# v's projection in pairs with its weight halves side by side, h's weights formed with fewer copies, identity products in the tail

## The reference

```python
v = relu(x @ Wv + bv); q = relu(x @ Wq + bq); k = relu(x @ Wk + bk)
att = softmax(q @ k.T * mask - NEG * (1 - mask))
x1 = layernorm(x + relu((att @ v) @ Wo + bo))

h = x1 @ W_w.T + W_b
e, f = h @ a1, h @ a2
u = adj * exp(e[:, None] + f[None, :] + a_b)
out = layernorm(x1 + (u / u.sum(-1)) @ h)
```

## Time and profile before

| | us |
|---|---|
| median of three runs | 425.09 |
| lowest, highest | 424.24, 425.4 |
| the profiled execution | 424.09 |
| its span on the core | 422.4 |
| TensorE / VectorE / ScalarE / GpSimd busy | 396.3 / 348.4 / 336.8 / 266.7 |

### The profile page before, as it was taken

The page is one execution under the profiler, slowest core; times in us unless marked ns, Lnnn a source line. Parts: engine busy times, 40 slices in busy tenths (PEclk is TensorE's granted clock), DMA queues, the critical chain, the costliest instruction groups (busy, mean ns, idle before and its releaser), DMA issues.

```text
span 422.4 us, 8762 instructions
## 1 busy us (share of the span) xinstructions
PE 396.3 (94%) x2812; PEld 367.5 (87%) x2812; DVE 348.4 (82%) x1002; ACT 336.8 (80%) x642; POOL 266.7 (63%) x230
## 2 busy tenths in 40 slices
PE   8789999999999999999999999999999999998580
PEld 7668998899999999999999999999999989988480
DVE  4595789879869896989869996989969999898755
ACT  5375767998789896998789987998789788985753
POOL 2453446456709698497929697496929893751862
PEclk9889999999999999999999999999999999999666
DMA  8940472626781657726792657726592768226661
GB/s 290 372 151 2 139 238 71 229 60 215 276 298 52 222 190 252 285 67 215 270 326 73 225 204 257 264 81 219 199 330 71 248 184 267 100 83 184 209 174 50
DMA packets 37868, 80.71 MB, mean 191 GB/s; under 512 B 2752, under 2 KB 19264, under 8 KB 37824
## 3 DMA queue, kind: packets, MB, share of 16 engines
q1 hardware_dynamic: 37680, 80.03, 55.1%
q10 hardware_dynamic: 144, 0.14, 0.2%
HBM read 75.96 MB, written 4.19 MB: 190 GB/s over the span
## 4 chain that ended last, share of the span: by engine, by line
PE 76%; DVE 11%; ACT 3%; issue 3%; DMA 2%; POOL 1%; ACTq 0%; DVEq 0%; POOLq 0%
PE pt_ps L1415 11%; PE m_ps L1463 10%; PE av_ps L1427 7%; PE av_ps L1428 7%; PE av_ps L1429 7%; PE s_ps L1356 6%; PE s_ps L1358 6%; PE s_ps L1357 6%; PE m_ps L1363 4%; PE m_ps L1356 3%; PE m_ps L1358 3%; PE m_ps L1357 3%; DVE prob L920 3%; DMA adjt_in<-in_adj_t_dram 2%; PE m_ps L1364 2%
## 5 line engine op out<-in xcount | busy, mean ns | idle before, releaser
L622 ACT ACTIVATE prob_th<-pt_ps 128x512 fp32r<-128x512 f32 x128 | 74.5, 593 | 30.8 <-PE pt_ps L1415 30.4
L928 DVE TENSOR_TENSOR prob_tl<-pt_ps,prob_th 128x512 fp32r<-128x512 f32 x128 | 85.7, 682 | 16.2 <-ACT prob_th L622 15.8
L920 DVE CUSTOM_DVE_ANT_0 prob<-s_ps,penalty 128x1024 f32<-128x1024 f32 x64 | 78.1, 1220 | 16.4 <-issue 6.5
L614 ACT ACTIVATE prob<-prob,neg_max 128x1024 f32<-128x1024 f32 x64 | 73.5, 1149 | 14.9 <-DVE neg_max L920 14.9
L379 POOL TENSOR_SCALAR penalty<-adj_in 128x1024 bf16<-128x1024 f32 x64 | 66.6, 1053 | 15.7 <-DVE neg_max L920 9.1
L1415 PE MATMUL pt_ps<-ident,prob 128*128 128x128 f32 x512 | 74.7, 275 | 0.0
L1427 PE MATMUL av_ps<-prob_th,vh 128*128 128x256 f32 x256 | 74.4, 291 | 0.0
L1429 PE MATMUL av_ps<-prob_th,vl 128*128 128x256 f32 x256 | 72.4, 283 | 0.0
L1428 PE MATMUL av_ps<-prob_tl,vh 128*128 128x256 f32 x256 | 72.4, 283 | 0.0
L572 ACT ACTIVATE adj_t<-adjt_in 128x1024 fp32r<-128x1024 f32 x58 | 61.1, 1054 | 9.2 <-DMA adjt_in<-in_adj_t_dram 7.5
L1415 PEld LDWEIGHTS pt_ps<-ident,prob 128*128 128x128 f32 x512 | 60.1, 142 | 7.1 <-issue 0.4
(11 more groups left out here) (132 smaller groups left out, 928.4 us busy)
## 6 DMA issues: line engine op xcount, KB each, us to landing
adj_in<-in_adj_dram SPq DMA_DIRECT2D x64, 512.0 KB, 5.1
adjt_in<-in_adj_t_dram SPq DMA_DIRECT2D x64, 512.0 KB, 4.3
xt_in<-in_x_t_dram SPq DMA_DIRECT2D x16, 256.0 KB, 4.2
x_in<-in_x_dram SPq DMA_DIRECT2D x8, 512.0 KB, 4.7
out_dram<-out_sb SPq DMA_DIRECT2D x14, 256.0 KB, 5.4
out_dram<-out_sb SPq DMA_DIRECT2D x4, 128.0 KB, 1.8
wb<-in_pack_b_dram SPq DMA_DIRECT2D x1, 320.0 KB, 4.1
wa<-in_pack_a_dram ACTq DMA_DIRECT2D x1, 132.0 KB, 3.7
```

Source lines behind the costliest of these rows:

```text
L614: sc.activation(prob[i % 2][:, :], prob[i % 2][:, :], ACT.Exp, bias=neg_max[:, i:i + 1], scale=-1.0, accum_out=row_sum[b % 2][:, i:i + 1]) ...
L622: sc.activation(prob_th[n % 2][:, tiles(k), (i % 2) * P:(i % 2 + 1) * P], pt_ps[k][:, :].rearrange("p (c n) -> p c n", n=P), ACT.Copy).the ...
L920: v.tensor_tensor_reduce(out=prob[i % 2][:, :], in0=s_ps[:, :, :].rearrange("p a n -> p (a n)"), in1=penalty[:, n % RING, :], scale=-1.0, ...
L928: v.tensor_tensor(prob_tl[n % 2][at], pt_ps[k][:, :].rearrange("p (c n) -> p c n", n=P), prob_th[n % 2][at].bitcast(F32), ALU.subtract).th ...
```

## The change

- v's projection works with `product_side_by_side` on four banks of two blocks each, instead of two banks of four blocks with three matmuls per block. VectorE's `v_out` adds bias to the low half (into `v_low`) and then the sum of both into the bank, and a new `v_relu` on ScalarE writes `vf` from the bank. v is now the reference's, so `bo_full` is bo itself, and the third product of `form_w1`, `minus_bv` and `bv_wide` are gone.
- The identity is built inside `rhs1`; `w1h` and `w1l` are formed straight from the bank.
- `hold_clock` issues six products of the identity with itself, at two places of TensorE's tail.
- The orders of all five queues and of the three banks are written anew for head, pass and tail. x is loaded for batch p in pass p rather than a pass ahead.

```diff
-            def project_v(b, k):
-                pe.wait_ge(*lower(xtl_done, b, k))
-                vv = shared("v", b, k)
-                for c in range(TH):
-                    t = k * TH + c
-                    last = product(blk(vv, c), (blk(xth, t), blk(xtl, t)), (wvh, wvl))
+            def project_v(b, j):
+                pe.wait_ge(*lower(xtl_done, b, j // 2))
+                vv = shared("v", b, j)
+                for c in range(2):
+                    t = 2 * j + c
+                    last = product_side_by_side(vv[:, c * PAIR:(c + 1) * PAIR], (blk(xth, t), blk(xtl, t)), flat(w_hl[:, 2, :, :]), D)
                 last.then_inc(v_full, 1)
...
-                v.tensor_tensor(half(vf, k)..., bank["v", b, k]..., rows(minus_bv[:, :], TH), ALU.max).then_inc(v_evac, 1)
+                v.tensor_tensor(v_low[:, :, :], vv[:, :, 1, :], rows(bv_row, 2), ALU.add).then_inc(v_biased, 1)
+                dve.wait_ge(v_biased, TH * b + j + 1)
+                v.tensor_tensor(vv[:, :, 0, :], vv[:, :, 0, :], v_low[:, :, :], ALU.add).then_inc(v_summed, 1)
...
+            def v_relu(b, j):
+                wait(act, vl_done, 2 * (b - 1) + j // 2 + 1)
+                act.wait_ge(v_summed, TH * b + j + 1)
+                sc.activation(vf[:, j * PAIR:(j + 1) * PAIR]..., vv[:, :, 0, :], ACT.Relu).then_inc(v_evac, 1)
...
             def place_rhs1():
-                dve.wait_ge(ident_ok, 2)
-                v.tensor_copy(rhs1[:, 0:D], ident[:, :]).then_inc(rhs_ok, 1)
+                dve.wait_ge(wa_arrived, 16)
                 v.tensor_copy(rhs1[:, D:E1], wa[:, A1:A2 + 1]).then_inc(rhs_ok, 1)
                 v.tensor_copy(wb_wide[:, :], wa[:, WB:WB + 1].broadcast_to([P, P])).then_inc(rhs_ok, 1)
-                v.tensor_copy(bv_wide[:, :], wa[:, BV:BV + 1].broadcast_to([P, P])).then_inc(rhs_ok, 1)
...
             def split_w1():
-                v.tensor_copy(w1f[:, :], av_ps[:, 0:E1]).then_inc(w1_ok, 1)
+                v.tensor_copy(w1h, av_ps[:, 0:E1]).then_inc(w1_ok, 1)
                 v.tensor_copy(wb_row[:, :], av_ps[:, E1:E1 + D]).then_inc(w1_ok, 1)
                 v.tensor_copy(beta2[:, :], av_ps[:, E1 + D:2 * E1]).then_inc(w1_ok, 1)
-                v.tensor_tensor(bo_full[:, :], av_ps[:, 2 * E1:2 * E1 + D], bo_row, ALU.add).then_inc(w1_ok, 1)
-                v.tensor_copy(w1h, w1f[:, :]).then_inc(w1_ok, 1)
+                v.tensor_tensor(w1l, av_ps[:, 0:E1], w1h.bitcast(F32), ALU.subtract).then_inc(w1_ok, 1)
...
+            def hold_clock():
+                pe.wait_ge(ptl_done, 2 * T * B - 1)
+                for _ in range(HOLD):
+                    pe.matmul(pt_ps[0][:, 0:P], ident, ident, start=True, stop=True)
...
             def head():        # TensorE
                 project_q(0, 0)
                 project_k(0, 0)
                 project_k(0, 1)
-                project_q(0, 1)
+                form_w1()
                 project_v(0, 0)
                 project_v(0, 1)
-                form_w1()
+                project_q(0, 1)
                 scores(0, 0)
-                project_v(1, 0)
+                project_v(0, 2)
+                project_k(1, 0)
                 scores(0, 1)
...
             def head():        # VectorE
                 split_qk()
                 first_x_lo(0)
                 first_x_lo(1)
+                place_rhs1()
                 split_vo()
...
-                split_w1()
                 mask_max(0, 2)
...
                 mask_max(0, 3)
+                split_w1()
+                v_out(1, 1)
...
             def tail():        # TensorE
+                transpose_x1(LAST, 0)
+                attend(LAST, 3)
                 project_h(LAST, 0)
                 project_h(LAST, 1)
+                aggregate(LAST - 1, 6)
+                aggregate(LAST - 1, 7)
                 project_h(LAST, 2)
+                hold_clock()
+                project_out(LAST, 3)
                 project_h(LAST, 3)
                 transpose_x1(LAST, 1)
...
                 aggregate_early(0)
                 aggregate_early(1)
+                hold_clock()
                 aggregate_early(2)
```

More of the change, by code:

```diff
@@ L754, in batch_pass @@
-                prob_hi(p, 2, 0)
-                probs(p, 3)
+                k_out(p + 1, 0)
                 if there(p - 2):
                     round_adj(p - 2, 5)
+                q_hi(p + 1, 0)
+                prob_hi(p, 2, 0)
+                if there(p - 2):
+                    round_adj(p - 2, 6)
+                probs(p, 3)
+                k_out(p + 1, 1)
                 prob_hi(p, 2, 1)
                 if there(p - 2):
-                    round_adj(p - 2, 6)
+                    round_adj(p - 2, 7)
@@ L789, in batch_pass @@
+                prob_hi(p, 6, 1)
                 probs(p, 7)
-                if there(p + 2):
-                    x_hi(p + 2, 1)
-                prob_hi(p, 6, 1)
-                g_hi(p - 1, 0)
+                g_hi_den(p - 1)
+                v_relu(p + 1, 2)
             def tail():
-                exp_ef(LAST - 2, 1)
+                av_hi(LAST - 1, 2)
+                g_hi(LAST - 2, 1)
+                prob_hi(LAST - 1, 7, 0)
+                q_out(LAST, 1)
+                v_relu(LAST, 3)
@@ L893, in _, with v_out @@
             v = nc.vector
-            def v_out(b, k):
-                wait(dve, vl_done, 2 * (b - 1) + k + 1)
-                dve.wait_ge(v_full, 2 * b + k + 1)
-                v.tensor_tensor(half(vf, k).rearrange("p (t d) -> p t d", d=D),
-                                bank["v", b, k][:, :].rearrange("p (t d) -> p t d", d=D),
-                                rows(minus_bv[:, :], TH), ALU.max).then_inc(v_evac, 1)
+            def v_out(b, j):
+                if b == 0 and j == 0:
+                    dve.wait_ge(wb_arrived, 16)
+                wait(dve, v_summed, TH * b + j)
+                dve.wait_ge(v_full, TH * b + j + 1)
+                vv = bank["v", b, j][:, :].rearrange("p (t a d) -> p t a d", a=2, d=D)
+                v.tensor_tensor(v_low[:, :, :], vv[:, :, 1, :], rows(bv_row, 2), ALU.add).then_inc(v_biased, 1)
+                dve.wait_ge(v_biased, TH * b + j + 1)
+                v.tensor_tensor(vv[:, :, 0, :], vv[:, :, 0, :], v_low[:, :, :], ALU.add).then_inc(v_summed, 1)
             def first_x_lo(k):
@@ L1129, in batch_pass @@
             def batch_pass(p):
+                if there(p - 2):
+                    g_lo_den(p - 2)
                 if there(p - 3):
@@ L1284, in tail @@
                 agg_out(LAST - 1, 1)
+                shift_mean0(LAST, 0)
+                agg_out(LAST - 1, 2)
+                prob_lo(LAST, 6, 1)
+                agg_out(LAST - 1, 3)
+                prob_lo(LAST, 7, 0)
+                av_lo(LAST, 2)
+                agg_out(LAST - 1, 4)
+                prob_lo(LAST, 7, 1)
                 o_out(LAST, 2)
                 residual0(LAST, 2)
+                agg_out(LAST - 1, 5)
+                x1_lo(LAST, 0)
+                h_out(LAST, 0)
@@ L1560, in batch_pass @@
                 transpose_p(p, 0, 1)
+                if there(p - 2):
+                    aggregate(p - 2, 0)
                 attend(p - 1, 3)
-                project_k(p + 1, 0)
                 scores(p, 2)
@@ L1576, in batch_pass @@
                 transpose_p(p, 2, 0)
-                scores(p, 4)
                 transpose_p(p, 2, 1)
-                attend(p, 0)
-                if there(p - 2):
-                    aggregate(p - 2, 3)
+                project_k(p + 1, 1)
                 if there(p - 2):
                     aggregate(p - 2, 4)
+                scores(p, 4)
+                if there(p - 2):
+                    aggregate(p - 2, 5)
                 transpose_p(p, 3, 0)
                 if there(p - 2):
-                    aggregate(p - 2, 5)
+                    aggregate(p - 2, 6)
@@ L1587, in batch_pass @@
                 if there(p - 2):
-                    aggregate(p - 2, 6)
+                    aggregate(p - 2, 7)
+                project_v(p + 1, 0)
+                project_v(p + 1, 1)
+                scores(p, 5)
                 transpose_p(p, 3, 1)
                 transpose_x1(p - 1, 0)
-                scores(p, 5)
+                attend(p, 0)
                 transpose_p(p, 4, 0)
-                if there(p - 2):
-                    aggregate(p - 2, 7)
-                transpose_p(p, 4, 1)
@@ L1605, in batch_pass @@
                 transpose_p(p, 5, 1)
[L1606 removed]
+                project_h(p - 1, 7)
                 scores(p, 7)
[L1608 removed]
+                project_out(p, 0)
+                project_v(p + 1, 2)
                 transpose_p(p, 6, 0)
+                transpose_p(p, 6, 1)
+                project_v(p + 1, 3)
+                attend(p, 2)
                 project_q(p + 1, 1)
[L1611 to L1612 removed]
```

663 lines of the change are left out of this document (321 added, 342 removed), and 9 rows, old and new, of tables (HEAD_SLOTS, PASS_SLOTS).

## The result

The changed kernel takes 419.85 us (median of four runs, 418.63 to 420.71) against 424.95 of the kernel before on the same chip: ratio 0.9879, 95% interval 0.9847 to 0.9912. Forecast were 412.5 and a range up to 419.5. It is faster, by 5.1 us instead of 12.6 (424.95 and 425.09 as the start), and 0.35 us outside the range. The profiled execution is the slowest of the four (420.71, span 419.0); a second one of the same kernel, in the experiments, has a span of 417.7.

A forecast was written before the change was run, and what follows sets the result against it. TensorE's instruction count times spacing was taken to bound the middle passes, with idling and half speed in the head. 424.1 - 7.5 (head) - 5.0 (passes) - 0 (tail) = 411.6, plus 1.0 for the median, said as 412.5; range 407 to 419.5.

The forecast's parts named there:

- The head, both steps: Start to pass 1: first scores 3.6 us earlier, then 3.9 us less from there to pass 1; 7.5 in all.
- the second wait: Head, TensorE's 2.1 us wait for a mask-and-maximum result; what is left of 3.4 us lost to half speed comes behind it.
- v's products: Passes 1 to 6 on TensorE: 0.46 us per bank, 0.84 less per batch, 5.0 us in all, range 3.7 to 5.9.
- So I cost them at nothing: Passes: VectorE's and ScalarE's 1.5 us more each priced at 0 while TensorE bounds, up to 1.0 us per pass for the range.
- rival A: Passes: denser VectorE and ScalarE hold TensorE up by 1 us in each, 418.5 us; chance 0.17.
- The sum of VectorE: VectorE's busy time per pass: 1.5 us more for v's operations, to 42.5 us.
- Pass 1: First of the six passes that form v of later batches: 40.3 us forecast, from 41.1 before.
- The tail: From the last batch's first scores to the end: 0 change, range 3 us slower to 4 faster.
- Rival C: Tail: the identity products do hold the clock, chain and sums run at full speed, some 4 us, 408.5; chance 0.10.
- B: Head gives only its first part, as a stall and half-speed stretch form elsewhere in it: 416.4 us; chance 0.10.
- D: Passes: late release of v's banks makes TensorE stand 2 us or more, half speed follows; 3.7 us each, 434.5; chance 0.04.

The follow-up runs named there:

- before, rhs early: Kernel before, with only the right-hand factor of h's weights placed ahead of VectorE's work on the second weight half in the head: 418.91 us, ratio 0.9854.
- the dose: Kernel before with the right-hand factor of h's weights early, plus four more VectorE operations per pass whose results nothing reads: 420.98 us, ratio 0.9907.
- the one with the old orders: Kernel before in nearly its own order, with the right-hand factor early and v's weight halves side by side in twice the banks: 460.91 us, ratio 1.0835.

## Why the prediction was wrong

- **The head, both steps: right.** 12.1 instead of 11.5 and 33.5 instead of 33.9. The early factor alone gives 5.3 of the 7.3 us by its first scores, and 6.4 by its time. That the half speed followed on stalls holds: without the first, none of it is left. The prediction tied a part of it to the second wait; in "before, rhs early" that wait stays and this part is gone too. The first copy's 1.1 us was read as its own: two of the four copies were held by GpSimd.
- **v's products: right.** 0.44 us per bank, and 46.47 us for a full pass without waits. The sum is also borne out, 46.4 to 46.5 where it was 47.3, so the measured distance was the right one to take, as the prediction did over the 81 ns that the Trainium skill (TensorE: Matmul & The Clock Gate, Back-to-back issue gap) gives. An estimate of the gain by that figure is 24 x 0.081 - 4 x 0.40 = 0.3 us per batch, rather than the 0.4 that the prediction has.
- **"So I cost them at nothing": this step failed.** I reasoned that VectorE and ScalarE keep 3.8 us of idle time in a pass and that this is enough. VectorE did keep 3.9, and its first mask of the pass was late by 0.65 us all the same: idle time lies where the engine waits for others, not ahead of the result that is wanted. In the old order the dose is nearly free (0.2 us a pass). In the new one taking away 1.7 us of v's sums gives 0.85 us a pass, and taking away the two small operations 0.75; both remove the 0.65 at the first mask. Another 0.5 us a pass, behind row tiles 2 and 3, stays in both, and its cause is open. The effect is rival A's (1 us in each pass), in its size too: 1.2 to 1.6 us over the bare products in passes 3 to 6 of the second execution. I had given it a chance of 0.17.
- **Within that step, a term was missing.** The sum of VectorE was 42.5 and became 43.8. v's operations were priced nearly right (0.41 and 0.43 against 0.40). The rest are two operations of eight numbers that were moved under GpSimd's, 1.7 us longer together than in the kernel before. Moving them to GpSimd brings VectorE to 42.3 and gives 0.65 to 0.75 us a pass. I read only the groups that the change names, not those it moves.
- **Pass 1** was to gain 0.8 and gained 0: TensorE is busy 0.6 us less there, and idles 0.5 us more.
- **The tail: 0 forecast, 2.0 lost**, inside the range that I gave it. 0.7 is the hold (1.3 per call was its price for TensorE, part of it in a stretch that waits anyway). The clock in the stretch without work fell as I had said. The other 1.3 us belong to the new order; which step of it costs them was not shown.
- Rival C didn't come about (clock 0.70 in the stretch it spoke of), B neither. D did not in this kernel; in the one with the old orders its late releases came, at twice its price and without a wait of 2 us.

How the loss would divide under the best order for this amount of work stays open: three orders were tried, not searched.

## What to carry to other kernels

When an edit moves work from the engine that bounds to one which is at 87% in a written order, don't price it by that engine's idle share. Ask what of the new work stands ahead of the next result that the bounding engine waits for: here 0.65 us of lateness sat at one mask. To find such a place, compare the distances between the same matmuls in two passes. Do the edits one by one before a reordering: an early right-hand factor alone, three small copies moved and a fourth saved, gave as much as the whole change. And look in both traces for operations whose duration differs though they don't.

## What the runs showed of the hardware

- A VectorE operation on 128x8 with two operands in SBUF takes 0.16 to 0.17 us with nothing of GpSimd beside it, and 1.02 to 1.09 when it begins just after an addition or conversion of GpSimd, with which it ends. A copy of 128x2 took 0.16 and 1.03. Beside GpSimd's reciprocal root one on 128x4 took 0.17. The same work on GpSimd takes 0.2 us an operation.
- One wait of 2.8 us near the start, taken away, gave 5.3 us by the first scores of pass 1. A wait of 2.1 us at a full clock was followed by half speed (29.3 to 32.6) in the kernel before, and by none in the one without the first wait.
- Twelve records of identity products ahead of a stretch of 7.25 us without work didn't keep the clock up behind it: it was at 0.50 from 390.6 to 400.7, and for as long without them.
- Four banks of v a pass, handed from VectorE to ScalarE among three shared ones, with the rest of the order nearly as it was, took a pass from 47.3 to 53.9 us.
